# The sum of the experts' output biases: one product of 48 rows a tile in place of two of 16

## The reference, cut to what matters

```python
xn = layernorm(x)                                        # x: 6250 nodes x 256
x = x + relu(gnn(xn, 100000 edges, 16 relations)) + mix(xn)   # graph sum and linear attention
t = layernorm(x)
logits = t @ router_w.T                                  # 8 experts
rw, re = top_k(softmax(logits), 2); rw = rw / rw.sum()
combine = zeros(N, 8).at[rows, re].set(rw)
for e in range(8):
    h = gelu(t @ w1[e] + b1[e])
    y = h @ w2[e] + b2[e]
    out = out + combine[:, e:e+1] * y                    # out starts at t
x = x + out
```

## Time and profile before

| | |
|---|---|
| median of three runs | 1849.27 us |
| the profiled execution's own time | 1848.28 us |
| its span, first to last instruction | 1846.5 us |
| outside the span | 1.78 us |
| TensorE busy | 1787.1 us, 97% of the span |
| VectorE busy | 1174.2 us, 64% |
| ScalarE busy | 772.5 us, 42% |
| GpSimd busy | 776.1 us, 42% |
| share of TensorE in the chain that ended last | 92% |

### The profile page before, as it was taken

The page is one execution under the profiler, slowest core; times in us unless marked ns, Lnnn a source line. Parts: engine busy times, 40 slices in busy tenths (PEclk is TensorE's granted clock), DMA queues, the critical chain, the costliest instruction groups (busy, mean ns, idle before and its releaser), DMA issues.

```text
span 1846.5 us, 30572 instructions
## 1 busy us (share of the span) xinstructions
PE 1787.1 (97%) x11137; PEld 1600.8 (87%) x11137; DVE 1174.2 (64%) x3496; ACT 772.5 (42%) x1428; POOL 776.1 (42%) x812
## 2 busy tenths in 40 slices
PE   7999999999999799999699999999999999999998
PEld 5887888888888699998689999999999998999998
DVE  6555555444444666767558677677776867767764
ACT  5555666555554433332124333343343332433443
POOL 2000000000000366667776666666666666666700
PEclk8999999999999999999999999999999999999999
DMA  7665777755555574444433433433334343343400
GB/s 227 239 234 204 278 288 282 265 216 217 217 217 202 209 306 150 143 131 126 149 113 107 135 112 109 131 98 121 109 112 133 98 123 111 98 134 105 120 26 17
DMA packets 113914, 296.06 MB, mean 160 GB/s; under 512 B 18120, under 2 KB 73792, under 8 KB 104420
## 3 DMA queue, kind: packets, MB, share of 16 engines
q1 hardware_dynamic: 75236, 189.63, 27.6%
q0 software_dynamic: 38528, 104.46, 19.3%
HBM read 162.70 MB, written 131.32 MB: 159 GB/s over the span
## 4 chain that ended last, share of the span: by engine, by line
PE 92%; DVE 3%; POOL 2%; issue 1%; ACT 1%; DMA 1%; SPq 0%; DVEq 0%; ACTq 0%
PE bank L51 23%; PE bank L53 22%; PE bank L52 22%; PE bank L1346 18%; PE bank L1335 2%; POOL plain L590 2%; PE bank L1411 1%; PE bank L1239 1%; PE bank L1451 1%; DMA plain<-messages,idxT 1%; PE bank L1214 1%; PE bank L1401 1%; PE bank L1392 1%; DVE parts L620 0%; DVE plain L958 0%
## 5 line engine op out<-in xcount | busy, mean ns | idle before, releaser
L590 POOL DMA_INDIRECT plain<-messages,idxT x784 | 765.3, 976 | 966.9 <-issue 825.5
L51 PE MATMUL bank<-parts 128*128 128x512 f32 (+2 forms) x2232 | 812.7, 364 | 9.9 <-DVE plain L991 5.0
L53 PE MATMUL bank<-parts 128*128 128x512 f32 (+2 forms) x2232 | 785.9, 352 | 0.0
L52 PE MATMUL bank<-parts 128*128 128x512 f32 (+2 forms) x2232 | 784.7, 352 | 0.0
L51 PEld LDWEIGHTS bank<-parts 128*128 128x128 f32 x2232 | 425.4, 191 | 59.8 <-DVE plain L991 6.0
L53 PEld LDWEIGHTS bank<-parts 128*128 128x128 f32 x2232 | 423.6, 190 | 55.2
L52 PEld LDWEIGHTS bank<-parts 128*128 128x128 f32 x2232 | 425.4, 191 | 46.8
L1346 PE MATMUL bank<-plain 128*128 128x128 f32 x3136 | 389.6, 279 | 23.1 <-DMA plain<-messages,idxT 19.4
L1346 PEld LDWEIGHTS bank<-plain 128*128 128x128 f32 x3136 | 374.8, 195 | 29.8 <-DMA plain<-messages,idxT 21.9
L1165 ACT ACTIVATE plain<-bank,small 128x512 f32<-128x512 f32 (+1 forms) x208 | 135.3, 663 | 372.2 <-PE bank L53 368.9
L663 DVE TENSOR_SCALAR plain<-bank,plain 128x256 f32<-128x256 f32 x392 | 171.0, 478 | 164.5 <-PE bank L53 110.9
(11 more groups left out here) (150 smaller groups left out, 987.6 us busy)
## 6 DMA issues: line engine op xcount, KB each, us to landing
messages<-plain SPq DMA_DIRECT2D x49, 2048.0 KB, 7.0
parts<-xnT_scratch SPq DMA_DIRECT2D x20, 1024.0 KB, 5.3
xnT_scratch<-parts SPq DMA_DIRECT2D x98, 128.0 KB, 3.3
plain<-messages,idxT POOLq DMA_INDIRECT x784
w_parts<-parts SPq DMA_DIRECT2D x32, 256.0 KB, 2.4
parts<-w_parts SPq DMA_DIRECT2D x4, 2048.0 KB, 20.6
plain<-in_x SPq DMA_DIRECT2D x48, 128.0 KB, 7.0
plain<-in_x SPq DMA_DIRECT2D x10, 512.0 KB, 4.3
```

The costliest lines, as they stand in the source:

```text
L51: e.matmul(out, left(0), right(0), start=start, stop=False)
L52: e.matmul(out, left(0), right(1), start=False, stop=False)
L53: return e.matmul(out, left(1), right(0), start=False, stop=stop)
L590: e.indirect_dma_start(msg[:, b % SLOTS, j, :], None, table_rows, bass.IndirectOffsetOnAxis(idxT[:, j, b:b + 1], 0)).then_inc(s_gather[b % ...
```

## The change: what it does, and the diff

Both sides get the four terms in rows of one operand. `b2_p` has 48 rows and one set of 256 columns: rows 0 to 15 hold the high parts of b2 (twice 8), rows 32 to 47 the low parts (twice 8), rows 16 to 31 zero. `comb_p` has 64 columns a tile: 8 high, 8 low and 16 zero columns, and that once more; 48 of them are transposed. One product of 48 rows then has all four terms. GpSimd clears both tiles at the start, ahead of its DMAs, and loads b2 four times (eight small DMAs, so both waits are for eight). ScalarE makes two casts of b2 in place of one. VectorE's low part of b2 is made on partitions 32 to 47, and its two writes of `comb_p` are twice as wide. The chain of the 13 `turn_choice` and 13 `bias` steps keeps its places in the order.

```diff
+    SIDE = 32
+    CHOICE = SIDE + 2 * X
-        b2_p = parts.carve(2, D)
-        comb_p = parts.carve(GROUP, 2, X)
+        b2_p = parts.carve(D)
+        comb_p = parts.carve(GROUP, 2, SIDE)
-        b2_rows = small_rows[0:2 * X, 1, D:2 * D]
+        b2_rows = small_rows[0:CHOICE, 1, D:2 * D]
 # GpSimd, start
+            e.memset(raw(b2_p)[0:CHOICE, :], 0.0).then_inc(s_zero_sides, 1)
+            e.memset(raw(comb_p), 0.0).then_inc(s_zero_sides, 1)
             for o, i in (...
-                         ..., (b2_rows[0:X], b2), (b2_rows[X:2 * X], b2)):
+                         ..., (b2_rows[0:X], b2), (b2_rows[X:2 * X], b2),
+                         (b2_rows[SIDE:SIDE + X], b2), (b2_rows[SIDE + X:CHOICE], b2)):
                 e.dma_start(o, i).then_inc(s_rows_in, 16)
 # VectorE, start
                     e.wait_ge(s_b2_high, 1)
-                    low(lambda i: b2_p[0:2 * X, i, :], b2_rows).then_inc(s_b2_low, 1)
+                    e.tensor_tensor(b2_p[SIDE:CHOICE, :], b2_rows[SIDE:CHOICE], raw(b2_p)[SIDE:CHOICE, :],
+                                    ALU.subtract).then_inc(s_b2_low, 1)
 # VectorE, route
-                e.tensor_copy(comb_p[:, 0:K, 0, :], combB[:, g % 2, 0, 0:K, :]).then_inc(s_top2, 1)
+                e.tensor_copy(comb_p[:, 0:K, :, 0:X], combB[:, g % 2, 0, 0:K, :].unsqueeze(2).to_broadcast([P, K, 2, X])).then_inc(s_top2, 1)
-                e.tensor_tensor(comb_p[:, 0:K, 1, :], combB[:, g % 2, 0, 0:K, :], raw(comb_p)[:, 0:K, 0, :],
-                                ALU.subtract).then_inc(s_comb_low, 1)
+                e.tensor_tensor(comb_p[:, 0:K, :, X:2 * X], combB[:, g % 2, 0, 0:K, :].unsqueeze(2).to_broadcast([P, K, 2, X]),
+                                raw(comb_p)[:, 0:K, :, 0:X], ALU.subtract).then_inc(s_comb_low, 1)
 # ScalarE, start
-                    e.wait_ge(s_rows_in, 16 * 6)
-                    e.copy(b2_p[0:2 * X, 0, :], b2_rows).then_inc(s_b2_high, 1)
+                    e.wait_ge(s_rows_in, 16 * 8)
+                    e.wait_ge(s_zero_sides, 2)
+                    e.copy(b2_p[0:2 * X, :], b2_rows[0:2 * X])
+                    e.copy(b2_p[SIDE:CHOICE, :], b2_rows[SIDE:CHOICE]).then_inc(s_b2_high, 1)
 # ScalarE, turn_choice
-                    e.copy(combT[0:2 * X, 0:n], bank[3][0:2 * X, 0:n]).then_inc(s_misc, 1)
+                    e.copy(combT[0:CHOICE, 0:n], bank[3][0:CHOICE, 0:n]).then_inc(s_misc, 1)
 # TensorE, start
-            e.wait_ge(s_rows_in, 16 * 6)
+            e.wait_ge(s_rows_in, 16 * 8)
 # TensorE, turn_choice
-                    m = e.transpose(bank[3][0:2 * X, k * P:(k + 1) * P], raw(comb_p)[:, k, :, :].rearrange("p i x -> p (i x)"),
-                                    ident[:, :])
+                    m = e.transpose(bank[3][0:CHOICE, k * P:(k + 1) * P],
+                                    raw(comb_p)[:, k, :, :].rearrange("p i x -> p (i x)")[:, 0:CHOICE], ident[:, :])
 # TensorE, bias
-                        for i in range(2):
-                            m = e.matmul(y_bank(y_use[g, X], p)[:, (k % 2) * D:(k % 2 + 1) * D], combT[0:2 * X, k * P:(k + 1) * P],
-                                         b2_p[0:2 * X, i, :], start=i == 0, stop=i == 1)
+                        m = e.matmul(y_bank(y_use[g, X], p)[:, (k % 2) * D:(k % 2 + 1) * D], combT[0:CHOICE, k * P:(k + 1) * P],
+                                     b2_p[0:CHOICE, :], start=True, stop=True)
```

More of the change, by code:

```diff
@@ L362, in gps_layer @@
         s_gather = [sem(f"gather{i}") for i in range(SLOTS)]
-        s_pool_const = sem("pool_const")
+        s_pool_const, s_zero_sides = sem("pool_const"), sem("zero_sides")
         s_x_pad, s_ln_stats, s_ln_sqrt, s_ln_rstd, s_xn = (sem(n) for n in ("x_pad", "ln_stats", "ln_sqrt", "ln_rstd", "xn"))
@@ L570, in pool_program @@
             e.memset(ones1[:, :], 1.0).then_inc(s_pool_const, 1)
+            e.memset(raw(b2_p)[0:CHOICE, :], 0.0).then_inc(s_zero_sides, 1)
+            e.memset(raw(comb_p), 0.0).then_inc(s_zero_sides, 1)
             for o, i in ((gate_rows, w_gate.rearrange("r f a -> r (f a)")), (router_rows, w_router),
                          (bout_rows, b_out.rearrange("(h p) -> h p", p=P)),
-                         (b1_rows, b1.rearrange("x (h p) -> (x h) p", p=P)), (b2_rows[0:X], b2), (b2_rows[X:2 * X], b2)):
+                         (b1_rows, b1.rearrange("x (h p) -> (x h) p", p=P)), (b2_rows[0:X], b2), (b2_rows[X:2 * X], b2),
+                         (b2_rows[SIDE:SIDE + X], b2), (b2_rows[SIDE + X:CHOICE], b2)):
                 e.dma_start(o, i).then_inc(s_rows_in, 16)
```

## The result

The changed kernel takes 1842.58 us (median of 8 runs, 1840.40 to 1847.24), the one before 1848.93 us in the same company (8 runs, 1847.20 to 1849.43). The ratio is 0.9968, with a 95% interval of 0.9959 to 0.9976: 5.9 us less, between 4.4 and 7.6 us. It was faster, as forecast, and the forecast of 1844.0 us (5.3 us less) lies inside the interval.

A forecast was written before the change was run, and what follows sets the result against it. TensorE was taken to bound the kernel; -5.9 us (products), +0.24 us (VectorE) and +0.30 us (start) gave -5.3 us, from a median of 1849.27 to 1844.0 us. The range for 8 in 10 was 1841.6 to 1846.6 us.

The forecast's parts named there:

- What bounds: Bias-step stretch: TensorE is the path, busy 831.1 of 835 us, so time saved there comes off the end.
- The products: Bias steps: 49 of 98 products go, each worth 0.12 us whatever its rows, -5.9 us.
- The break: TensorE's standstill around each bias step, 0.38 us a group, 4.9 us in all: unchanged at 48 rows, 0 us.
- rival (a): Bias steps: the standstill goes too at 48 rows, -10.2 us in all, 1839.1 us; chance 0.10.
- The transposes: Before the bias products: 49 transposes of 48 columns cost the same as of 16, 0 us.
- VectorE: Routing chain: two wider writes add 0.06 us a group, on the path in 4 places, +0.24 us.
- Rival (b): Four groups where TensorE waits for line 991: VectorE's backlog takes 1.9 us back, 1845.9 us; chance 0.15.
- The start: Kernel start: ScalarE's second cast of b2 adds +0.30 us to the chain, between 0 and 0.40 us.
- Rival (c), the late rows: Start: the eight small DMAs land late, TensorE starts 4.1 us later at lower clock, 1854.4 us; chance 0.05.
- a sign that I had named: Start: the small transposes would still stand at about 14.4 us in the chain.
- The forecast's own range: Whole kernel: 1843.0 to 1845.2 us, from the product's bounds (-0.5 to +0.5) and the start; chance 0.70.

The follow-up runs named there:

- experiment 2: The kernel before without the product with the low parts of b2, so one product of 16 rows a tile; ratio 0.9987 against the kernel before.
- experiment 9: The changed kernel with each tile's product of 48 rows issued nine times, operands laid out for 128 rows; ratio 1.0274 against the kernel before.
- experiment 10: The changed kernel with nine products of 128 rows a tile in place of one of 48; ratio 1.0191 against the kernel before.
- experiment 6: The changed kernel with products of 128 rows in place of 48, second run of it; ratio 0.9984 against the kernel before.
- experiment 1: The kernel before with only the changed kernel's start (clears, eight small DMAs, second cast of b2); ratio 1.0014 against the kernel before.

## Why the prediction was right

- **What bounds.** TensorE's work in the stage was the path. The links fell by 0.47 us (full) and 0.35 us (small), its wait for VectorE grew by only 0.1 us, and the 810 us from the first to the twelfth step became shorter by 4.55 us, at a granted clock of 1.00 in both kernels. Shown.
- **The products, -5.9 us.** The links give 10 x 0.47 + 3 x 0.35 = 5.75 us. A product costs 0.12 us at 16, 48 and 128 rows: experiments 2, 9 and 10. Shown by links; the time of experiment 10 agrees. From the first to the twelfth step the profiles differ by 4.55 us and the links by 10 x 0.47 + 0.35 = 5.05 us. Most of the half microsecond seems to stand in the edge batches: of those with 16 products in that part of the chain, 11 take 1.86 to 1.89 us in the changed kernel and 5 before, where 1.78 us is usual. What slows them isn't known.
- **The break, 0.** Unchanged at 48 rows (4.3 us of standstill, 13 times, in both), and rival (a) is what happens at 128: -0.40 us a group, where 0.38 us was worked out. Shown by links, not by time.
- **The transposes, 0.** Four of the 48-column transposes take 0.44 us in the chain, as four of 16 columns did, and four of 128 columns take 0.44 us in experiment 6 as well. Shown.
- **VectorE, +0.24 us.** Line 973 (the former 966) takes a median of 196 ns instead of 181 ns, line 975 (968) 224 ns instead of 192 ns: 0.05 us a group for 0.06 us. TensorE's wait grew by 0.1 us. Rival (b) didn't come: VectorE waits for TensorE ahead of its routing chain 12 times, as before.
- **The start, +0.30 us.** Too small for the link: the casts' link grew from 0.30 us to 0.75 us (17.47 - 16.72). It took in the second cast's full 0.40 us, where the first was left after 0.31 us. The link is 0.45 us longer, and the range's end was 0.40 us. Timeline of ScalarE in the changed kernel:
```profile
16.63 0.40 ACT L1107 CAST parts<-plain 16x256 fp32r<-16x256 f32 x1
17.04 0.40 ACT L1108 CAST parts<-plain 16x256 fp32r<-16x256 f32 x1
17.47 1.14 ACT L1100 CAST parts<-plain 128x512 fp32r<-128x512 f32 x2
```
  What of it reaches the end isn't shown. The chain carries a delay of 1.66 us on to TensorE's products of line 1239 (now 1248) at 26 to 28 us, and at the next ones of that line, at 41 us, 0.15 us is left. Between them TensorE ran at half clock for fewer products in the changed kernel: products of 0.23 us follow from 31.87 us on, against 32.82 us before. Chain of waits, before and then changed:
```profile
26.07 1.03 PE bank L1239 x4
41.05 0.35 PE bank L1239 x4
```
```profile
27.73 0.71 PE bank L1248 x4
41.20 0.35 PE bank L1248 x4
```
- **Rival (c), the late rows.** Not seen: ahead of the small transposes TensorE's loads stand still for 0.4 us as before, with all eight DMAs in. But the small transposes came at 15.56 us and not at about 14.4 us, a sign that I had named and that failed. The clock rose late: in the changed kernel the first products ran at half clock until about 14.6 us, before until 12.33 us. In experiment 1, which has the same start, the transposes came 1.0 us sooner than in the changed kernel. So I take that as chance; two or three executions can't prove it.

The sum by measured terms: -5.75 + 0.1 + 0.45 = -5.2 us with the start's link in full, -5.5 us with the 0.15 us that is left of it at 41 us; both lie inside the interval of 4.4 to 7.6 us less. The interval is too wide to tell the small terms from nothing. The forecast's own range isn't what its named terms give. A bound of -0.5 us on the products stands in none of the workings, and the products' +-0.5 us with the start's -0.3 and +0.1 us give 1843.2 to 1844.6 us and not 1843.0 to 1845.2 us. The median of 1842.58 us lies under both, though the kernel before was 0.3 us faster in that company too.

## What to carry to other kernels

Where TensorE is the path, a product of few rows costs what one of all rows costs (here 0.12 us for 256 columns at 16, 48 and 128 rows), so terms that share an output should be stacked in rows and summed by one product. Pad such a product to the row count of its neighbours when the operands allow it: here the 0.40 us around each narrow step comes to 5.2 us by the links, nearly as much as the 49 products, though no time of a whole kernel resolved it. When a profile's difference is a few microseconds, cut both traces at events that the change doesn't touch, and look at the granted clock in each piece, before a gain or a loss is put down to the change.

## What the runs showed of the hardware that was not expected

Long steps of products of few rows were at times followed by a lower granted clock, where the same steps with 128 rows were not. Behind 4.49 us of back-to-back products of 48 rows the clock was 0.50 to 0.57 over 4 us in 5 of 13 groups; in three of them the step itself had run at 1.00 and without a standstill. Behind 4.31 us of products of 128 rows it was 1.00 in all 13. Behind steps of 0.55 to 1.14 us, as in the kernels before and after, it was 1.00 in all 13 too. With 48 and 128 rows by turns, or 16 and 48, it fell inside nearly every step, but there the weight loads stood still at each change of rows, so the rows and the standstills can't be told apart. Why 5 groups fell and 8 didn't is open.

The change of rows has a price of its own: 0.19 us at full clock for each change between 48 and 128 rows, and the same kind of standstill between 16 and 48. And a kernel that took 1849 us in one company took 1995 to 2011 us in three others, with standstills on several engines that the profile puts to no known cause; what they are is open.
